# Four exact blocks of a Q piece instead of two, with the order of a slot rewritten on three engines

## The chip, the core and the metric

The kernel runs on one core of one Trainium2 chip. The metric is the device time of one launch in microseconds. A core has a tensor engine (TensorE, PE; its weight loads are PEld), a vector engine (VectorE, DVE), a scalar engine (ScalarE, ACT), GpSimd (POOL), and a sync engine (SyncE, SP) whose only work here is to issue DMAs. Each works through its own list of instructions in order and waits on semaphores.

## What is computed

One decoder layer with quantised weights on x of 2 x 512 x 1024:

```
x = x + attn(layernorm(x))      # 32 heads of 128, 8 KV heads, rope, causal softmax
                                # q, k, v, o weights: (codes - 8) * scales, one scale per 128 rows and column
x = x + fake_quant(layernorm(x)) @ fake_quant(ctx)    # ctx 2 x 1024 x 1024, 8 bit codes
x = x + layernorm(x) @ binarised(weight)              # sign(w) * mean|w| - clip(w) + clip(w)
```

A fp32 product is made of fp16 halves: each operand is split into an upper and a lower half, and three products (upper x upper, upper x lower, lower x upper) are summed. The codes minus 8 are small whole numbers and exact in one fp16. A product with unscaled codes therefore takes two matmuls instead of three, but its scale has to be applied to the result.

## The kernel before

Attention runs in 64 slots. A slot is one head and one batch row: p = 0 to 63, with i = p mod 8 inside the group g of one KV head, h = i // 2 the head and b = i % 2 the batch. The slots overlap as a pipeline written out by hand: in slot p the engines make the scores and the softmax of slot p, Q for slot p + 2, the weighted values of slot p - 1, and the output projection (O) of earlier heads. Every engine's list of a slot is one function called slot (POOL's is body), and the order of calls in it is the schedule. No scheduler stands between.

TensorE in a slot, in 128 x 512 matmuls: scores in three units u = 0, 1, 2 (3 + 3 + 1.5 columns' worth), Q for p + 2 from eight 128-row blocks, three units of O and one of the slot before (16 matmuls), and weigh, the product with V (7.5). For Q, q_exact multiplies with bare codes (2 matmuls), q_base lets ScalarE multiply the partial sum in PSUM by the ratio of this block's scale to the next one's, and so on; q_part adds the rest, each block with three matmuls of scaled halves. Two blocks are exact. The ratios stand in o_now, which o_scales copies from o_table; ratio_step computes the table once, in the K phase before the slots.

A piece of Q's weights is 128 x 512, half a head. It is loaded to stage_c (codes) and stage_s (scales broadcast). VectorE's piece_scale multiplies them, ScalarE's piece writes the upper half to w_a, VectorE's piece_lo the lower half. The exact columns of the first piece of a head need only (code - 8).

Q's result goes this way: ScalarE q_copy to SBUF, POOL q_turn (times cosine), ScalarE q_swap (two copies that exchange the partition halves), POOL sine, VectorE q_sum, ScalarE q_hi, POOL q_lo; then the scores can start.

The softmax of a slot: VectorE maxima after each score unit, ScalarE exps, VectorE two reciprocals (row_inv: three columns, then the fourth), POOL norm on four parts, ScalarE prob_split in two parts, POOL prob_rest, four transposing DMAs, TensorE weigh a slot later, ScalarE ao_part and VectorE ao_rest. O's results are added to x_acc by VectorE (o_add), four a slot; two PSUM tiles take turns, so a unit waits for the add two before it.

Beside that, slots 8 to 39 turn ctx into codes: ScalarE scales to uint8 and subtracts 128 in a second instruction. Slots 40 to 62 prepare the ffn weights (wf_upper and wf_sign on ScalarE, wf_lower and wf_difference on VectorE, wf_clip and wf_add on POOL). After slot 63 come the rest of O, the cross product and the ffn.

The groups 1 to 4 are a hardware loop on TensorE, VectorE, POOL and SP (each_group); on ScalarE they are written out.

## Time and profile before

| what | value |
|---|---|
| median of 3 runs | 1050.04 us (1050.01 to 1050.68) |
| profiled execution | 1050.22 us |
| its span | 1048.4 us |
| PE busy | 1015.7 us, 97%, 5296 matmuls |
| DVE busy | 902.7 us, 86% |
| POOL busy | 788.9 us, 75% |
| ACT busy | 774.4 us, 74% |
| granted TensorE clock | 1.000 |

The span is from the first to the last instruction of the profiled execution. A busy share says how much of the span an engine executed; it doesn't say where it is waited for. In the forty slices of the page TensorE has nine tenths or more in all but the first. Its slots lie between 168 us (first score product) and 895 us (last).

### The profile page before, as it was taken

The page shows a single profiled execution, that of the slowest core. Times are in us where ns is not written, and L with a number is a line of the kernel's source. Part 1 is how long each engine was busy: PE and PEld are TensorE (multiplying, and loading weights), DVE is VectorE, ACT ScalarE, POOL GpSimd, SP SyncE. Part 2 cuts the span into 40 slices and gives each one's busy share as a digit, 9 for nine tenths or more (in the row PEclk, how much of TensorE's full clock was granted, in tenths as well). Part 3 has the DMA queues.
Part 4 walks back from the last instruction along what each step waited for, and adds up shares of the span by engine and source line. Part 5 has one row for each costly group of instructions (what it writes and reads, how often), then busy time and mean ns, then how long its engine had stood idle before and what let it go on. Part 6 is the DMA issues. An engine that isn't in the chain of part 4 may idle for free.

```text
span 1048.4 us, 18487 instructions
## 1 busy us (share of the span) xinstructions
PE 1015.7 (97%) x5296; PEld 500.5 (48%) x5296; DVE 902.7 (86%) x1651; ACT 774.4 (74%) x1712; POOL 788.9 (75%) x833
## 2 busy tenths in 40 slices
PE   5999998999999999999999999999999999989998
PEld 3444343445555555555555455545555554454443
DVE  7989997699888888888888889999999998887773
ACT  5547766888898888888888888888888887473210
POOL 3678787899878887887888789999999999332200
PEclk9999999999999999999999999999999999999999
DMA  9783301676887676667667766777787765534442
GB/s 337 258 199 121 116 26 34 145 152 157 161 162 166 138 165 158 147 152 159 165 138 165 157 147 140 153 165 150 156 150 156 160 138 113 118 122 96 88 96 74
DMA packets 309804, 152.01 MB, mean 145 GB/s; under 512 B 257728, under 2 KB 274240, under 8 KB 309728
## 3 DMA queue, kind: packets, MB, share of 16 engines
q1 hardware_dynamic: 301952, 137.76, 58.0%
q10 hardware_dynamic: 7776, 13.37, 4.5%
q8 instruction: 31, 0.51, 0.2%
q14 instruction: 45, 0.37, 0.1%
HBM read 85.26 MB, written 4.19 MB: 85 GB/s over the span
## 4 chain that ended last, share of the span: by engine, by line
PE 82%; DVE 6%; POOL 5%; ACT 3%; issue 2%; DMA 1%; ACTq 0%; SPq 0%; DVEq 0%; POOLq 0%
PE out_ps L969 10%; PE proj_ps L969 9%; PE side_ps L949 9%; PE side_ps L757 8%; PE side_ps L759 8%; PE side_ps L758 8%; PE side_ps L845 5%; PE proj_ps L1130 5%; PE score_ps L932 3%; PE score_ps L933 3%; PE score_ps L934 3%; PE proj_ps L1135 2%; PE score_ps L1100 2%; PE out_ps L780 1%; PE proj_ps L757 1%
## 5 line engine op out<-in xcount | busy, mean ns | idle before, releaser
L1687 POOL TENSOR_SCALAR prob<-prob,row_inv 128x512 f32<-128x512 f32 (+3 forms) x256 | 196.7, 779 | 81.9 <-DVE row_inv L2224 80.3
L1694 POOL TENSOR_TENSOR w_b<-prob,w_b 128x896 f16<-128x896 f32 (+2 forms) x192 | 186.0, 995 | 6.5 <-ACT w_b L1373 6.4
L1346 ACT ACTIVATE prob<-score_ps,neg_max 128x512 f32<-128x512 f32 (+3 forms) x256 | 132.9, 526 | 30.7 <-DVE neg_max L2141 29.1
L2154 DVE SCALAR_TENSOR_TENSOR x_acc<-out_ps,o_now,x_acc 128x1024 f32<-128x1024 f32 x120 | 153.1, 1276 | 1.3 <-PE out_ps L969 1.3
L2154 DVE SCALAR_TENSOR_TENSOR x_acc<-proj_ps,o_now,x_acc 128x1024 f32<-128x1024 f32 x120 | 153.0, 1275 | 0.0
L757 PE MATMUL side_ps<-hT,w_a 128*128 128x512 f16 x384 | 145.5, 379 | 0.5 <-ACT side_ps L1313 0.2
L759 PE MATMUL side_ps<-hT,w_a 128*128 128x512 f16 x384 | 145.5, 379 | 0.0
L758 PE MATMUL side_ps<-hT,w_a 128*128 128x512 f16 x384 | 145.5, 379 | 0.0
L2141 DVE CUSTOM_DVE_ANT_0 score_ps<-score_ps,mask_b 128x512 f32<-128x512 f32 (+3 forms) x256 | 122.7, 501 | 16.9 <-PE score_ps L934 16.6
L969 PE MATMUL proj_ps<-work,w_b 128*128 128x512 f16 x496 | 127.3, 379 | 1.9 <-DVE x_acc L2154 1.5
L969 PE MATMUL out_ps<-work,w_b 128*128 128x512 f16 x496 | 127.3, 379 | 0.8 <-DVE x_acc L2154 0.7
L949 PE MATMUL side_ps<-work,v_sb 128*128 128x512 f16 (+3 forms) x768 | 114.8, 299 | 0.2 <-DMA work<-w_b 0.2
L1900 DVE SCALAR_TENSOR_TENSOR w_a<-stage_s,w_a 128x256 f16<-128x256 f32 (+1 forms) x64 | 64.7, 1010 | 43.4 <-ACT w_a L1216 43.1
L1373 ACT ACTIVATE w_b<-prob 128x896 f16<-128x896 f32 (+2 forms) x192 | 99.3, 550 | 3.6 <-POOL prob L1687 1.6
L1313 ACT ACTIVATE side_ps<-side_ps,o_now 128x512 f32<-128x512 f32 x120 | 79.3, 661 | 27.8 <-PE side_ps L845 24.3
L1682 POOL TENSOR_TENSOR swapped<-swapped,sin_t 128x512 f32<-128x512 f32 x77 | 99.7, 1295 | 0.0
L949 PEld LDWEIGHTS side_ps<-work,v_sb 128*128 128x128 f16 (+1 forms) x768 | 69.6, 98 | 45.3 <-DMA work<-w_b 1.2
L932 PE MATMUL score_ps<-k_sb,q_sb 128*128 (+4 forms) x256 | 76.7, 299 | 3.6 <-ACT prob L1346 2.0
L1707 POOL TENSOR_TENSOR q_sb<-rot,q_sb 128x512 f16<-128x512 f32 x62 | 78.9, 1273 | 0.0
L969 PEld LDWEIGHTS proj_ps<-work,w_b 128*128 128x128 f16 x496 | 48.2, 98 | 60.2 <-DVE x_acc L2154 2.5
L969 PEld LDWEIGHTS out_ps<-work,w_b 128*128 128x128 f16 x496 | 48.3, 98 | 59.7 <-DVE x_acc L2154 2.0
L933 PE MATMUL score_ps<-k_sb,q_sb 128*128 (+4 forms) x256 | 76.6, 299 | 0.0
(276 smaller groups left out, 2230.1 us busy)
## 6 DMA issues: line engine op xcount, KB each, us to landing
stage_c<-in_codes_dram SPq DMA_DIRECT2D x72, 256.0 KB, 2.9
stage_o<-in_codes_dram SPq DMA_DIRECT2D x64, 256.0 KB, 3.3
stage_s<-in_scales_dram SPq DMA_DIRECT2D x34, 256.0 KB, 3.7
ctx_raw<-in_ctx_dram ACTq DMA_DIRECT2D x32, 256.0 KB, 3.2
work<-w_b SPq DMA_TRANSPOSE x261, 3.1
x_acc<-in_x_dram SPq DMA_DIRECT2D x8, 512.0 KB, 8.9
k_sb<-in_codes_dram SPq DMA_DIRECT2D x16, 256.0 KB, 7.0
v_sb<-in_scales_dram SPq DMA_DIRECT2D x16, 256.0 KB, 7.4
```

The costliest lines, as they stand in the source:

```text
L757: pe.matmul(o, stat(0), mov(0), start=first, stop=False, skip_group_check=onto)
L758: pe.matmul(o, stat(0), mov(1), start=False, stop=False, skip_group_check=onto)
L759: return pe.matmul(o, stat(1), mov(0), start=False, stop=last, skip_group_check=onto)
L932: pe.matmul(o, q[0], k[0], start=True, stop=False)
L933: pe.matmul(o, q[0], k[1], start=False, stop=False)
L949: mm = pe.matmul(pv_ps[:, kb * P:S], v_sb[:, bass.ds(g, 1), l, b * TB + kb, :].rearrange("p a d -> p (a d)"), probT[:, m, at:kb + (TB - 1) ...
L969: mm = pe.matmul(o[:, b, :], o_codes[:, h % RING, cb * P:(cb + 1) * P], ao[:, h % 2, l, b * S:(b + 1) * S], start=l == 0, stop=l == 1)
L1346: ins = act.activation(prob[:, SCORE_AT[qb]:SCORE_AT[qb] + w], score_ps[:, score_bank(i, u), off:off + w], ACT.Exp, bias=neg_max[:, c:c + ...
L1687: return pool.tensor_scalar(prob[:, at:at + w], prob[:, at:at + w], row_inv[:, col:col + 1], P_UP, ALU.mult, ALU.mult)
L1694: ins = pool.tensor_tensor(prob16[:, 1, to:to + w], prob[:, at:at + w], prob16[:, 0, to:to + w], ALU.subtract)
L2141: ins = dve.tensor_tensor_reduce(s, s, mask_b[:, S - w:S], -1.0, MAX_FROM, ALU.add, ALU.min, neg_max[:, c:c + 1])
L2154: ins = dve.scalar_tensor_tensor(y, u, s, y, ALU.mult, ALU.add)
```

## The change

It raises the exact blocks of a Q piece from two to four in the slots whose Q is that of slots 10 to 63; TensorE makes it in slots 8 to 61 (the function many). An even piece is then whole: all of its 512 columns are exact, so it needs no scales, no piece_scale and no piece_lo. In these slots:

- TensorE: four q_exact of two matmuls, and q_part over four blocks instead of six. The first score unit is parted after its second product, the O units are parted at two, three or one of their four matmuls.
- ScalarE: four q_base instead of two; the second context instruction has gone to VectorE; the exchange of Q's halves is parted: one half at the end of a slot behind both prob_splits, the other after the next slot's first q_base. The last exponential comes behind the fourth q_base, q_hi and o_cut.
- VectorE: the first O add and q_sum stand ahead of the third maxima and of the first reciprocal; in the context slots a tensor_scalar from uint8 to bf16 behind the second reciprocal.
- SP: for a whole piece one load instead of two, and a wait on piece_hi instead of piece_done.
- Ratios: three columns of ratios instead of one, in six steps (14 instructions instead of 11), held in ctx_raw.
- The groups 1 to 4 are written out on every engine.

TensorE at the start of a context slot, from the first score product, before (side_ps<-hT,w_a is Q, score_ps the scores, out_ps and proj_ps the O units):

```order
L932 MATMUL score_ps<-k_sb,q_sb 128x512
L933 MATMUL score_ps<-k_sb,q_sb 128x512
L934 MATMUL score_ps<-k_sb,q_sb 128x512
L845 MATMUL side_ps<-hT,w_a 128x512 x2
L969 MATMUL out_ps<-work,w_b 128x512 x4
L932 MATMUL score_ps<-k_sb,q_sb 128x384
L933 MATMUL score_ps<-k_sb,q_sb 128x384
L934 MATMUL score_ps<-k_sb,q_sb 128x384
L932 MATMUL score_ps<-k_sb,q_sb 128x128
L933 MATMUL score_ps<-k_sb,q_sb 128x128
L934 MATMUL score_ps<-k_sb,q_sb 128x128
L845 MATMUL side_ps<-hT,w_a 128x512 x2
```

and now:

```order
L972 MATMUL score_ps<-k_sb,q_sb 128x512 x2
L884 MATMUL side_ps<-hT,w_a 128x512 x2
L972 MATMUL score_ps<-k_sb,q_sb 128x512
L1008 MATMUL out_ps<-work,w_b 128x512 x4
L884 MATMUL side_ps<-hT,w_a 128x512 x2
L972 MATMUL score_ps<-k_sb,q_sb 128x384 x3
L972 MATMUL score_ps<-k_sb,q_sb 128x128 x3
L1008 MATMUL proj_ps<-work,w_b 128x512 x2
L884 MATMUL side_ps<-hT,w_a 128x512 x2
L1008 MATMUL proj_ps<-work,w_b 128x512 x2
L1008 MATMUL out_ps<-work,w_b 128x512 x3
L884 MATMUL side_ps<-hT,w_a 128x512 x2
```

The exact pairs (two matmuls to side_ps) went from two to four; between each pair and the next stand five 512-wide matmuls or as much.

VectorE from the first score unit's O add to the first reciprocal, in the weight stage before, an odd slot (ISA is the maxima instruction and its accumulator read, rot<-rot,swapped is q_sum, x_acc an O add):

```order
L2154 SCALAR_TENSOR_TENSOR x_acc<-out_ps,o_now,x_acc 128x1024
L2141 ISA score_ps,neg_max<-score_ps,mask_b 128x384
L2141 ISA neg_max 128x1
L2141 ISA score_ps,neg_max<-score_ps,mask_b 128x128
L2141 ISA neg_max 128x1
L2141 ISA score_ps,neg_max<-score_ps,mask_b 128x256
L2141 ISA neg_max 128x1
L2154 SCALAR_TENSOR_TENSOR x_acc<-proj_ps,o_now,x_acc 128x1024
L2224 RECIPROCAL row_inv<-row_sum 128x3
L2054 TENSOR_TENSOR rot<-rot,swapped 128x512
```

and in a context slot now; in the weight stage these rows are the same:

```order
L2250 SCALAR_TENSOR_TENSOR x_acc<-out_ps,o_now,x_acc 128x1024
L2237 ISA score_ps,neg_max<-score_ps,mask_b 128x384
L2237 ISA neg_max 128x1
L2237 ISA score_ps,neg_max<-score_ps,mask_b 128x128
L2237 ISA neg_max 128x1
L2250 SCALAR_TENSOR_TENSOR x_acc<-proj_ps,o_now,x_acc 128x1024
L2145 TENSOR_TENSOR rot<-rot,swapped 128x512
L2237 ISA score_ps,neg_max<-score_ps,mask_b 128x256
L2237 ISA neg_max 128x1
L2324 RECIPROCAL row_inv<-row_sum 128x3
```

The second O add and q_sum moved ahead of the third maxima (128x256) and the reciprocal.

ScalarE from the second probability split to the first scaling of the next slot's Q, before (an odd slot follows; swapped<-stage_o is half of the exchange, w_b<-prob the split, work<-side_ps the ao copy, side_ps<-side_ps q_base):

```order
L1221 ACTIVATE swapped<-stage_o 64x512
L1222 ACTIVATE swapped<-stage_o 64x512
L1373 ACTIVATE w_b<-prob 128x128
L1373 ACTIVATE w_b<-prob 128x256
L1382 ACTIVATE work<-side_ps 128x512
L1329 ACTIVATE o_now<-work 128x10
L1432 DMA ctx_raw<-in_ctx_dram 128x512
L1313 ACTIVATE side_ps<-side_ps,o_now 128x512
```

and now:

```order
L1447 ACTIVATE w_b<-prob 128x128
L1447 ACTIVATE w_b<-prob 128x256
L1370 ACTIVATE swapped<-stage_o 64x512
L1456 ACTIVATE work<-side_ps 128x512
L1506 DMA ctx_raw<-in_ctx_dram 128x512
L1387 ACTIVATE side_ps<-side_ps,o_now 128x512
L1370 ACTIVATE swapped<-stage_o 64x512
L1387 ACTIVATE side_ps<-side_ps,o_now 128x512
```

One half of the exchange stands between the second split and the ao copy, the other between the first and the second q_base; before, both stood ahead of the second split.

The diff, cut to its core:

```diff
-N_EXACT = 2
-EXACT = N_EXACT * P
+N_EXACT = 4
+FEW_EXACT = 2
+MANY = range(SLOTS + Q_AHEAD, N_SLOTS)
+def exact_of(p):
+    return N_EXACT if p in MANY else FEW_EXACT
+def whole(n):
+    return exact_columns(n) == PIECE
+        def many(p):
+            return p + Q_AHEAD in MANY
...
         def each_group(eng, body):
             body(0)
-            with eng.Fori(1, CTX_GROUPS + 1) as g:
+            for g in range(1, CTX_GROUPS + 1):
                 body(g, True)
...
+                if exact == PIECE:
+                    return
                 sp.dma_start(stage_s[:, r, exact:PIECE],
...
-                    sp.wait_ge(piece_done, p + FIRST_PIECES)
+                    of = p + FIRST_PIECES - 1
+                    sp.wait_ge(*((piece_hi, of + 1) if whole(of) else (piece_done, halved(of + 1))))
...
+                if many(p):
+                    scores(p, i, g, 0, range(2))
+                    q_exact(*ahead, 0)
+                    scores(p, i, g, 0, range(2, 3))
+                    o_unit(p - 1, prev[1], 3)
+                    q_exact(*ahead, 1)
+                    scores(p, i, g, 1)
+                    o_unit(p, i, 0, range(0, 2))
+                    q_exact(*ahead, 2)
+                    o_unit(p, i, 0, range(2, 4))
+                    o_unit(p, i, 1, range(0, 3))
+                    q_exact(*ahead, 3)
+                    o_unit(p, i, 1, range(3, 4))
+                    scores(p, i, g, 2)
+                    o_unit(p, i, 2, range(0, 2))
+                    q_part(*ahead, range(N_EXACT, KB))
+                    o_unit(p, i, 2, range(2, 4))
+                    weigh(p - 1, prev[1], prev[0])
+                    return
...
+                if whole(n):
+                    act.activation(w[:, 0, col:col + PIECE], stage_c[:, r, :], ACT.Copy, bias=-CODE_ZERO)\
+                        .then_inc(piece_hi, 1)
+                    return
...
+            def q_swap_half(p, half):
+                if half == 0:
+                    act.wait_ge(q_summed, p)
+                    act.wait_ge(q_copied, p - FIRST_PIECES + 1)
+                a, z = half * 64, half * 64 + 64
+                ins = act.activation(swapped[a:z, :], q_sum_in[64 - a:128 - a, :], ACT.Copy)
+                if half:
+                    ins.then_inc(q_swapped, 1)
...
+                if many(p):
+                    if many(p - 1):
+                        q_swap_half(p - 1 + Q_AHEAD, 1)
                     q_base(*next_q, 1)
+                    exps(p, i, 0)
+                    if i % B:
+                        o_scales(g, i)
+                    q_base(*next_q, 2)
+                    exps(p, i, 1)
+                    q_base(*next_q, 3)
                     q_hi(p + 1)
+                    o_cut(p, i)
+                    if wf_late(p) is not None:
+                        wf_upper(wf_late(p))
+                    exps(p, i, 2)
+                    if with_ctx:
+                        act.wait_ge(ctx_landed, q * 16 + 16)
+                        act.activation(ctx_codes, ctx_raw[:, :], ACT.Identity, scale=scal[:, 5:6],
+                                       bias=scal[:, 3:4]).then_inc(ctx_scaled, 1)
...
                 prob_split(p, 1)
+                if many(p):
+                    q_swap_half(p + Q_AHEAD, 0)
+                    if not many(p + 1):
+                        q_swap_half(p + Q_AHEAD, 1)
...
+                    dve.tensor_tensor(per[:, :, 0], rows[:, :, 0], per[:, :, 0], ALU.mult)
+                    ins = dve.tensor_tensor(per[:, :, 1:], by[:, :, 0:N_EXACT - 2], per[:, :, 1:], ALU.mult)
...
                 maxima(p, i, 1)
-                maxima(p, i, 2)
-                if has_o:
+                if many(p):
                     if i % B:
                         dve.wait_ge(o_now_ready, g * RF + i // B)
                     o_add(p, i, 0)
-                dve.wait_ge(exp_done, p * 3 + 2)
-                dve.reciprocal(row_inv[:, 0:3], row_sum[:, 0:3]).then_inc(inv_ready[0], 1)
-                if has_next and by_parts(p + 1):
                     q_sum(p + 1)
+                maxima(p, i, 2)
+                if many(p):
+                    dve.wait_ge(exp_done, p * 3 + 2)
+                    dve.reciprocal(row_inv[:, 0:3], row_sum[:, 0:3]).then_inc(inv_ready[0], 1)
...
-                if has_piece:
-                    piece_scale(n, i % 2, (EXACT, 0)[i % B])
+                if has_piece and not whole(n):
+                    piece_scale(n, i % 2, exact)
                 dve.wait_ge(exp_done, p * 3 + 3)
                 dve.reciprocal(row_inv[:, 3:4], row_sum[:, 3:4]).then_inc(inv_ready[1], 1)
+                if with_ctx:
+                    q, dst = ctx_half(g, i)
+                    dve.wait_ge(ctx_scaled, q + 1)
+                    dve.tensor_scalar(dst, ctx_codes, Q_MID, None, ALU.subtract).then_inc(ctx_free, 1)
```

## Rows read from the trace of the kernel before

**Rows 1.** Windows view, the context stage; busy us of each engine, clock, DMA.
```profile
466.00:558.00 92.00, 92.00 (x499) 46.71 (x498) 78.01 (x145) 81.62 (x186) 76.18 (x81) 1.00 0.68 155
```

**Rows 2.** Timeline of TensorE: start us, us, engine, line, operation, tiles.
```profile
697.72 0.38 PE L932 MATMUL score_ps<-k_sb,q_sb 128*128 128x512 f16 x1
709.18 0.38 PE L932 MATMUL score_ps<-k_sb,q_sb 128*128 128x512 f16 x1
510.97 1.03 PE L969 MATMUL out_ps<-work,w_b 128*128 128x512 f16 x4
```

**Rows 3.** Timeline of ScalarE, context stage; last row a group, mean ns.
```profile
508.11 0.48 ACT L1346 ACTIVATE prob<-score_ps,neg_max 128x256 f32<-128x256 f32 x1
508.56 0.82 ACT L1453 ACTIVATE ctx_raw<-ctx_raw,scal 128x512 uint8<-128x512 f32 x1
509.73 0.63 ACT L1321 ACTIVATE q_sb<-rot 128x512 f16<-128x512 f32 x1 [0.35 <-DVE rot L2054]
511.78 0.93 ACT L1373 ACTIVATE w_b<-prob 128x896 f16<-128x896 f32 x1
512.74 0.63 ACT L1221 ACTIVATE swapped<-stage_o 64x512 f32<-64x512 f32 x1
514.03 0.62 ACT L1373 ACTIVATE w_b<-prob 128x128 f16<-128x128 f32 x2
514.56 0.58 ACT L1382 ACTIVATE work<-side_ps 128x512 f16<-128x512 f32 x1
L1313 ACT ACTIVATE side_ps<-side_ps,o_now 128x512 f32<-128x512 f32 x64 | 42.4, 662 | 16.0 <-PE side_ps L845 12.5
```

**Rows 4.** Timeline of VectorE, context stage.
```profile
503.79 0.69 DVE L2170 SCALAR_TENSOR_TENSOR work<-side_ps,work 128x512 f16<-128x512 f32 x1 [0.40 <-ACT work L1382]
506.94 0.14 DVE L2141 DVE_READ_ACCUMULATOR2_ANT neg_max<- 128x1 f32 x1
507.40 0.43 DVE L2141 CUSTOM_DVE_ANT_0 score_ps<-score_ps,mask_b 128x256 f32<-128x256 f32 x1 [0.32 <-PE score_ps L934]
507.75 0.14 DVE L2141 DVE_READ_ACCUMULATOR2_ANT neg_max<- 128x1 f32 x1
509.03 0.66 DVE L2054 TENSOR_TENSOR rot<-rot,swapped 128x512 f32<-128x512 f32 x1
509.61 0.68 DVE L1894 SCALAR_TENSOR_TENSOR stage_s<-stage_c,stage_s 128x512 f32<-128x512 int32 x1
521.07 0.42 DVE L1894 SCALAR_TENSOR_TENSOR stage_s<-stage_c,stage_s 128x256 f32<-128x256 int32 x1
```

**Rows 5.** Timeline of POOL, an odd slot and the even one after it.
```profile
509.28 2.05 POOL L1687 TENSOR_SCALAR prob<-prob,row_inv 128x512 f32<-128x512 f32 x2 [2.24 <-DVE row_inv L2224]
511.30 1.15 POOL L1707 TENSOR_TENSOR q_sb<-rot,q_sb 128x512 f16<-128x512 f32 x1
513.67 2.90 POOL L1694 TENSOR_TENSOR w_b<-prob,w_b 128x896 f16<-128x896 f32 x3
520.75 1.78 POOL L1687 TENSOR_SCALAR prob<-prob,row_inv 128x512 f32<-128x512 f32 x2 [1.71 <-DVE row_inv L2224]
524.60 1.89 POOL L1694 TENSOR_TENSOR w_b<-prob,w_b 128x896 f16<-128x896 f32 x1
```

**Rows 6.** Groups of POOL, the two slots' first norm.
```profile
L1687 POOL TENSOR_SCALAR prob<-prob,row_inv 128x512 f32<-128x512 f32 x1 | 1.5, 1487 | 2.2 <-DVE row_inv L2224 2.2
L1687 POOL TENSOR_SCALAR prob<-prob,row_inv 128x512 f32<-128x512 f32 x1 | 1.2, 1220 | 1.7 <-DVE row_inv L2224 1.7
```

**Rows 7.** Groups of VectorE over the span.
```profile
L2080 DVE TENSOR_SCALAR q_ratio<-q_ratio 128x32 f32<-128x32 f32 x1 | 1.2, 1245 | 0.0
```

**Rows 8.** Groups of VectorE in the weight stage.
```profile
L2101 DVE SCALAR_TENSOR_TENSOR w_b<-w_b,wf_mean 128x256 f32<-128x256 f32 x15 | 19.3, 1289 | 0.0
L2107 DVE SCALAR_TENSOR_TENSOR w_b<-w_b 128x256 f16<-128x256 f32 x14 | 10.6, 758 | 0.0
L1900 DVE SCALAR_TENSOR_TENSOR w_a<-stage_s,w_a 128x512 f16<-128x512 f32 x7 | 6.6, 944 | 0.0
```

More of the change, by code:

```diff
@@ L59 @@
 Q_AHEAD = 2
-N_EXACT = 2
-EXACT = N_EXACT * P
+N_EXACT = 4
+FEW_EXACT = 2
+RATIO_STEPS = 6
 Q_LEAD = 3
@@ L852, in q_part @@
                 p = g * SLOTS + i
-                first = N_EXACT if by_parts(p) else 0
+                first = exact_of(p) if by_parts(p) else 0
                 if known(p) and p < Q_AHEAD and kbs[0] % 4 == 0:
@@ L1025, in slot @@
                 if has_ahead:
-                    q_part(*ahead, range(N_EXACT if parts else 3, KB))
+                    q_part(*ahead, range(exact_of(p + Q_AHEAD) if parts else 3, KB))
                 if has_o:
@@ L2081, in ratio_step @@
                 elif k == 2:
-                    ins = dve.tensor_tensor(by, by, rows[:, :, 1], ALU.add)
+                    ins = dve.tensor_tensor(by, by, of, ALU.add)
                 elif k == 3:
@@ L2181, in slot @@
                 n = p + FIRST_PIECES
+                exact = 0 if i % B else exact_columns(n)
                 p_ge2 = not (known(p) and p < 2)
```

172 lines of the change are left out of this document (95 added, 77 removed).

## The prediction, made before the result was known

> **What bounds the kernel now.** I read the table of windows first, because busy shares over the whole span mix stages. From 466 to 558 us, inside the context stage, TensorE is busy for 92.00 of 92.00 us and the granted clock is 1.00, which is the 2.4 GHz level; ScalarE stands at 81.62 and POOL at 76.18 [rows 1]. Then I read TensorE's timeline for the step of a slot: the first score product of one slot starts at 697.72, the next at 709.18, so a slot is 11.46 us [rows 2]. That is in the weight stage; in the context stage POOL's first norms stand as far apart (509.28 and 520.75) [rows 5]. Four matmuls issued in a row show as 1.03 us, of which the last one's own 0.38 is a modelled end, so a 512-wide matmul costs a step of (1.03 - 0.38) / 3 = 0.215 us [rows 2]. The slots are bound by TensorE's issue, and whatever goes from it comes back in full only if nobody else needs more than the shorter slot.
>
> **TensorE's part.** A block from exact codes takes two matmuls, any other three. Four instead of two exact blocks in 54 slots removes 54 x 2 matmuls: 108 x 0.215 = 23.2 us, 0.43 a slot, so a slot of pure issue would be 11.03 us. Each further exact block adds a scaling in place by ScalarE between two pairs of matmuls: 0.66 us [rows 3]. The new TensorE order puts five matmuls' worth (1.07 us) between the pairs, enough for the drain of the pair before (about 0.2 more than its issue) and 0.66, with about 0.1 to 0.2 us over. So the ladder costs nothing if ScalarE comes to each scaling on time. That is the condition to examine.
>
> **ScalarE's part.** In the window ScalarE is busy 81.62 / 92 x 11.46 = 10.17 us a slot [rows 1]. It gains 2 x 0.66, loses the second context copy (a step of 0.51, below) and, in half the slots, about 0.1 for a piece that is now one instruction instead of two: 10.9 of 11.03. It hardly has room to wait, and now it must wait for TensorE four times a slot. Beside that its half swap stands behind the second splitting of the probabilities: 0.63 [rows 3].
>
> **The loop that closes through VectorE, POOL and ScalarE.** I follow one round of an odd context slot, from ao_rest on VectorE to the ao_rest a slot later.
> Before: ao_rest, first maxima, O add, second maxima take 503.79 to 506.94 = 3.15, third maxima 0.35 (507.40 to 507.75), the next O add 1.20 (507.75 to 509.03, less the 0.08 of the reciprocal between): 4.70 [rows 4]. From there the reciprocal and its semaphore take 0.33 until POOL's first norm at 509.28 (0.08 to q_sum at 509.03, 0.25 more). POOL goes from that norm at 509.28 to the first subtraction at 513.67: 4.39 [rows 5]. ScalarE's second split takes 0.53 (514.03 to 514.56), the ao copy 0.58, semaphores 0.07 [rows 3]. Sum 10.60, which is 0.86 under the slot: nobody sees it.
> After: q_sum stands ahead of the third maxima and the reciprocal, +0.60 (0.66 less the usual overlap of 0.06) [rows 4]. The half swap stands between the split and the ao copy, +0.63, and +0.10 because a row before a swap keeps its full step (split at 511.78, 0.93 long, swap only at 512.74) [rows 3]. On the other side POOL's first norm no longer meets q_sum: q_sum ran until 509.69, so 0.41 of it lay on the norm, -0.41. Sum 11.52 for an odd slot. In an even slot, whose piece is whole, piece_scale and piece_lo are gone: POOL's stretch was already 0.54 shorter there (520.75 to 524.60 = 3.85) [rows 5] and loses 0.33 more of the scaling (from 521.16, where q_sum must end if it repeats the slot before, to 521.49) and, an estimate, 0.17 of piece_lo: 10.48, to which the new VectorE copy adds up to 0.5. The two kinds alternate. An even slot is then set by TensorE (11.03) or ScalarE's own round: q_sum's end at 3.15 + 1.20 + 0.66 = 5.01, four short copies (q_hi, o_cut, q_cut, q_copy) at the step of 0.51 that the four instructions from 509.73 to 511.78 show (2.05), exponential 0.45 (508.11 to 508.56), context scaling 0.73 (0.82 less an overlap of 0.1), splits 0.85 and 0.62, swap 0.63, ao 0.58: 10.92 [rows 3, 4]. Mean (11.52 + 11.03) / 2 = 11.28, and rounds that cross from one chain into the other can only lengthen it. I take 11.35 for the 32 slots with context, with 11.03 and 11.75 as ends.
>
> **Why I subtract port time.** The same norm of 128x512 took 1487 ns in one slot and 1220 in the next [rows 6]. The slots differ by VectorE's scaling of 512 or 256 columns (0.68 and 0.42 us, at 509.61 and 521.07 [rows 4]), and the difference of the norms, 267 ns, is that of the scalings. So POOL stands still while such a VectorE instruction runs. The Trainium skill ("GPSIMD Engine Reference", Key points) says that the two share SBUF interfaces and collide where VectorE has two SBUF inputs or a two-port mode; by that rule, the trace agrees: q_sum and the scalings have two SBUF inputs, and the O adds, one from PSUM, do no harm. The moved context copy has one SBUF source, so the rule catches it only in a two-port mode.
> The trace speaks for catching it: a tensor_scalar on 32 columns in SBUF took 1245 ns [rows 7], where 256 columns elsewhere take 0.42: it stood behind something as long as a two-input instruction of POOL (q_lo: 1.15 [rows 5]). The copy itself isn't in the trace of before. Its bounds: 0.42, the 256-wide row, and 1.8 us, 0.66 (q_sum, as wide) behind a q_lo of 1.15; I take 0.5. It hides behind the wait for the third exponential unless caught.
>
> **The 22 slots with ffn weights (40 to 61).** Here VectorE's in-order round counts. Front to q_sum's end 5.01 [rows 4]. Then the fourth part of the exponentials, which now stands behind q_hi: two short copies 1.02, wf_upper 0.35 (an estimate, from copies twice as wide at 0.51), exponential 0.48 with about 0.08 for its accumulator, semaphores 0.1: 7.04. VectorE waits for it at the second reciprocal (0.08), and only then does wf_lower 0.76, piece_lo 0.94 in half the slots (0.47), wf_diff 1.29 [rows 8], two O adds 2.40: 12.04. These durations contain waits for POOL; with 0.42 for each 256-wide one (the scaling of that width) and 0.66 for the lo they would give 10.69, below TensorE's 11.03. POOL is as loaded as before and its q_lo still falls on wf_lower, but wf_diff now meets short norms. I take 11.70, with ends 11.03 and 12.04.
>
> **The rest.** SP loads no scale rows for whole pieces: fewer transfers, and its transposes issue as before. The table of ratios makes 14 small VectorE instructions where there were 11, in a phase where VectorE is nearly full; the one of 1245 ns waited some 1.1 us for POOL [rows 7], and the steps go from seven to six: between -1 and +2, I take +0.5. Filling and leaving the stage: +0.5. That four engines' loops are written out costs nothing: the slots at 697 us are already straight code and have the same 11.46 step [rows 2].
>
> **Sum.** 32 x (11.35 - 11.46) = -3.5; 22 x (11.70 - 11.46) = +5.3; +1.0: +2.8 us. The profiled execution took 1050.2 (span 1048.4 and 1.8 around it), the median of the runs is 1050.04, so the two can be set equal: 1053 us. With 11.35 +- 0.12 and 11.70 +- 0.2 this case reaches from 1046 to 1061.
>
> **Rivals.**
> 1. TensorE stays the bound. For it: all loops have slack of 0.9 us or more before, and the even slots lose 0.9 us of VectorE work. Against it: the additions to the loop alone are 1.33. If every slot is 11.03, 1050.2 - 23.2 = 1027; if only the odd ones stay at 11.2 to 11.5, 1033 to 1045.
> 2. Slower outright, by one mechanism: VectorE, which comes late from the exponential, meets POOL's q_lo (1.15 us) with a port-holding instruction in each slot, the moved copy in the context slots, wf_lower in the others, and hands the lateness to the O adds and to ao_rest. Then context slots are 11.75 and weight slots 12.04: 32 x 0.29 + 22 x 0.58 = +22, 1072 us. It decides from the point where the second reciprocal starts after POOL has begun q_lo. By the Trainium skill's page named above this is what a two-port copy must do; by the rows it is open.
> 3. The gains meet the losses exactly: context slots at 11.2 and weight slots at 11.8 give -8.3 + 7.5 + 1 = 0, 1050. It lies inside the first case's range.
>
> **Chances.** The forecast with the third rival, 1046 to 1061: 0.50. Rival 1, 1027 to 1046: 0.31. Rival 2, above 1061: 0.19. Less than 0.2% (2.1 us) can't be told from no change. Of the forecast's 0.50, 0.06 is faster than 1048, 0.17 lies within 1047.9 to 1052.1, 0.27 above. So faster 0.37, same 0.17, slower 0.46. The range leaves out about one in ten on each side: 1037 to 1065.
>
> **What would show it.** In the profile after, TensorE should have holes of 0.1 to 0.7 us in the slots, most before the second exact pair (waiting for ScalarE's scaling of side_ps) or before an O unit (waiting for an O add of VectorE), and few in slots 0 to 7. The slot steps should alternate, or average 11.35 in the context stage and 11.7 in the weight stage. POOL's first norm should be nearer 0.7 than 1.22 us in even slots. VectorE should wait 1 us or more for the third exponential. I am wrong if TensorE is whole between 283 and 830 us (rival 1), or if the weight slots are no longer than the context slots. If the copy of the context codes on VectorE lasts over 1 us, rival 2's mechanism is there.

## The result, and the profile after

The changed kernel takes 1064.01 us (median of 4 runs, 1063.71 to 1064.15) beside 1050.24 for the kernel before on the same chip: a ratio of 1.013 with a 95% interval of 1.012 to 1.014. It is 1.3% slower. The prediction said 1053, with 1037 to 1065. The profiled execution has a span of 1062.4.

First the windows. The columns are window, length, then busy time and instructions of PE, PEld, DVE, ACT and POOL, granted clock, DMA share, GB/s. The first is the stretch of [rows 1], the second lies in the stage with ffn weights.

```profile
466.00:558.00 92.00, 89.68 (x484) 43.49 (x482) 78.27 (x145) 86.56 (x190) 73.07 (x81) 1.00 0.65 149
650.00:742.00 92.00, 86.53 (x462) 41.18 (x460) 79.46 (x143) 82.46 (x188) 78.85 (x94) 1.00 0.66 146
```

Where before TensorE was busy for all 92 us, it now lacks 2.3 in the context stage and 5.5 in the weight stage, at an unchanged clock of 1.00. (Over the whole page before, three slices besides the first stand at eight tenths, not nine; none of them lies inside these windows.) It no longer sets the slots. Its timeline says where the holes are: ahead of the second pair of exact matmuls, waiting for ScalarE's scaling in place.

```profile
518.32 0.61 PE L884 MATMUL side_ps<-hT,w_a 128*128 128x512 f16 x2 [0.58 <-ACT side_ps L1387]
...
715.88 0.60 PE L884 MATMUL side_ps<-hT,w_a 128*128 128x512 f16 x2 [0.71 <-ACT side_ps L1387]
```

The step of a slot can be read on ScalarE's ao copy, which comes once a slot. Five starts in the changed kernel, three of them in the context stage:

```profile
505.19 0.57 ACT L1456 ACTIVATE work<-side_ps 128x512 f16<-128x512 f32 x1
...
517.00 0.57 ACT L1456 ACTIVATE work<-side_ps 128x512 f16<-128x512 f32 x1
...
528.09 0.57 ACT L1456 ACTIVATE work<-side_ps 128x512 f16<-128x512 f32 x1
...
702.62 0.57 ACT L1456 ACTIVATE work<-side_ps 128x512 f16<-128x512 f32 x1
...
714.56 0.57 ACT L1456 ACTIVATE work<-side_ps 128x512 f16<-128x512 f32 x1
```

Context slots are 11.81 (odd) and 11.09 (even) in turn, 11.45 on average, where [rows 2, 5] had 11.46. Weight slots are 11.94 here and 12.07 for the next, 12.00 on average, against 11.46. Before slot 2 the ao copy already starts 1.9 us later (194.16 for 192.24). Followed through all ao copies, the lag behind the kernel before is 2.4 us at the end of slot 7, 2.3 at the end of slot 39, 13.6 at the end of slot 61 and 13.9 at the last one. So of the 14 us 11.3 come from the 22 weight slots, 1.9 from the phase that computes K with 0.4 in the slots just behind it, 0.3 from the end, and nothing from the 32 context slots. 22 x 0.54 would be 11.9; slot 40 is still 11.08, slot 60 is 11.45, and slot 61, the last of them, is 12.76 against 11.46.

What delays the scaling in an even weight slot is seen when the three other engines are laid side by side. VectorE, POOL and ScalarE from 708 us:

```profile
708.67 0.17 DVE L2324 RECIPROCAL row_inv<-row_sum 128x3 f32<-128x3 f32 x1
710.39 0.16 DVE L2339 RECIPROCAL row_inv<-row_sum 128x1 f32<-128x1 f32 x1 [1.54 <-ACT prob L1420]
710.47 1.20 DVE L2203 SCALAR_TENSOR_TENSOR w_b<-w_b 128x256 f16<-128x256 f32 x1
712.21 0.48 DVE L2197 SCALAR_TENSOR_TENSOR w_b<-w_b,wf_mean 128x256 f32<-128x256 f32 x1 [0.54 <-ACT w_b L1482]
```

```profile
709.01 1.25 POOL L1778 TENSOR_SCALAR prob<-prob,row_inv 128x512 f32<-128x512 f32 x2 [1.22 <-DVE row_inv L2324]
710.23 1.16 POOL L1798 TENSOR_TENSOR q_sb<-rot,q_sb 128x512 f16<-128x512 f32 x1
711.36 0.99 POOL L1778 TENSOR_SCALAR prob<-prob,row_inv 128x128 f32<-128x128 f32 x2
```

```profile
711.76 0.42 ACT L1482 ACTIVATE w_b<-w_b 128x256 f32<-128x256 f32 x1 [0.89 <-DVE w_b L2203]
712.08 0.58 ACT L1377 ACTIVATE stage_o<-side_ps 128x512 f32<-128x512 f32 x1
712.56 1.44 ACT L1447 ACTIVATE w_b<-prob 128x896 f16<-128x896 f32 x3
714.03 0.63 ACT L1370 ACTIVATE swapped<-stage_o 64x512 f32<-64x512 f32 x1
714.56 0.57 ACT L1456 ACTIVATE work<-side_ps 128x512 f16<-128x512 f32 x1
715.16 0.66 ACT L1387 ACTIVATE side_ps<-side_ps,o_now 128x512 f32<-128x512 f32 x1
```

wf_lower (L2203) starts 0.24 after POOL's q_lo (L1798) and ends only behind it: 1.20 us. ScalarE's next instruction, wf_sign (L1482), waits 0.89 for it, and behind wf_sign stand q_copy, the splits, the half swap, the ao copy and the scaling for which TensorE waits. The VectorE row at 712.21, wf_diff, was 1289 ns in [rows 8] and is 0.48 now: the contention has moved from it to wf_lower, where somebody waits.

In the context stage the odd and the even slot differ on POOL. The first and second batch of norms of an odd slot, then of an even one:

```profile
511.65 1.53 POOL L1778 TENSOR_SCALAR prob<-prob,row_inv 128x512 f32<-128x512 f32 x2 [2.09 <-DVE row_inv L2324]
...
514.28 1.51 POOL L1778 TENSOR_SCALAR prob<-prob,row_inv 128x128 f32<-128x128 f32 x2
...
523.40 1.25 POOL L1778 TENSOR_SCALAR prob<-prob,row_inv 128x512 f32<-128x512 f32 x2 [2.29 <-DVE row_inv L2324]
...
525.75 1.00 POOL L1778 TENSOR_SCALAR prob<-prob,row_inv 128x128 f32<-128x128 f32 x2
```

The second batch takes 0.5 longer in the odd slot. VectorE's new context copy reaches 0.3 us into it in both slots; what only the odd slot has is piece_lo, which lies wholly inside it:

```profile
513.42 1.16 DVE L2343 TENSOR_SCALAR v_sb<-ctx_raw 128x512 bf16<-128x512 uint8 x1 [0.54 <-ACT ctx_raw L1526]
514.50 0.68 DVE L1991 SCALAR_TENSOR_TENSOR w_a<-stage_s,w_a 128x512 f16<-128x512 f32 x1
...
525.17 0.88 DVE L2343 TENSOR_SCALAR v_sb<-ctx_raw 128x512 bf16<-128x512 uint8 x1 [0.54 <-ACT ctx_raw L1526]
```

Between 283 and 550 us the 24 copies lasted 1023 ns on average. Before 128 us, VectorE's third scaling of a piece and the wide reciprocal of the ratio table:

```profile
115.86 0.74 DVE L2174 RECIPROCAL ctx_raw<-ctx_raw 128x96 f32<-128x96 f32 x1
...
125.26 1.64 DVE L1985 SCALAR_TENSOR_TENSOR stage_s<-stage_c,stage_s 128x512 f32<-128x512 int32 x1
```

In the trace of before, that reciprocal on 32 columns took 0.34 and that scaling 0.67. Not all of the lag comes from there. VectorE's first rot<-rot,swapped, at 74.00 us before, stands at 74.45 now, ahead of the first step of the table, and between 73.96 and 74.66 in the traces of e1, e2, e8, e9 and e11. So 0.45 of the 1.9 is an earlier difference, not the table's.

### The profile page after: what moved, and what is told of

It is laid out like the page before. It is cut to its first block, busy times and chain, and to the rows that moved or that the text cites. A ratio compares the mean times of both kernels' runs of the same rounds, so it can differ in the third digit from the quotient of the medians.

```text
span 1062.4 us, 17456 instructions
## 1 busy us (share of the span) xinstructions
PE 1004.0 (95%) x5188; PEld 478.0 (45%) x5188; DVE 891.1 (84%) x1632; ACT 816.8 (77%) x1761; POOL 760.2 (72%) x833
## 4 chain that ended last, share of the span: by engine, by line
PE 48%; DVE 17%; ACT 12%; issue 11%; POOL 9%; ACTq 1%; DMA 1%; DVEq 0%; SPq 0%; POOLq 0%
PE proj_ps L1008 6%; PE side_ps L884 6%; PE score_ps L972 5%; PE proj_ps L1190 5%; POOL prob L1778 4%; PE side_ps L988 4%; PE out_ps L1008 4%; DVE x_acc L2250 3%; PE side_ps L796 2%; PE side_ps L798 2%; PE side_ps L797 2%; PE proj_ps L1195 2%; DVE score_ps L2237 2%; PE score_ps L1160 2%; DVE rot L2145 2%
## 5 line engine op out<-in xcount | busy, mean ns | idle before, releaser
L1778 POOL TENSOR_SCALAR prob<-prob,row_inv 128x512 f32<-128x512 f32 (+3 forms) x256 | 171.9, 682 | 103.2 <-DVE row_inv L2324 96.7
L1387 ACT ACTIVATE side_ps<-side_ps,o_now 128x512 f32<-128x512 f32 x228 | 150.9, 662 | 8.6 <-PE side_ps L884 3.5
L884 PE MATMUL side_ps<-hT,w_a 128*128 128x512 f16 x456 | 136.3, 381 | 22.4 <-ACT side_ps L1387 22.3
L972 PE MATMUL score_ps<-k_sb,q_sb 128*128 128x512 f16 (+3 forms) x768 | 144.6, 299 | 4.8 <-ACT prob L1420 3.8
L1008 PE MATMUL proj_ps<-work,w_b 128*128 128x512 f16 x496 | 145.9, 381 | 1.5 <-DVE x_acc L2250 1.5
L1008 PE MATMUL out_ps<-work,w_b 128*128 128x512 f16 x496 | 136.3, 380 | 2.0 <-DVE x_acc L2250 0.7
L796 PE MATMUL side_ps<-hT,w_a 128*128 128x512 f16 x276 | 104.5, 379 | 0.5 <-ACT side_ps L1387 0.2
L798 PE MATMUL side_ps<-hT,w_a 128*128 128x512 f16 x276 | 104.6, 379 | 0.0
L797 PE MATMUL side_ps<-hT,w_a 128*128 128x512 f16 x276 | 104.6, 379 | 0.0
L972 PEld LDWEIGHTS score_ps<-k_sb,q_sb 128*128 128x128 f16 x768 | 71.8, 98 | 65.4 <-ACT prob L1420 6.8
L988 PEld LDWEIGHTS side_ps<-work,v_sb 128*128 128x128 f16 x768 | 70.0, 98 | 46.1 <-issue 1.4
L884 PEld LDWEIGHTS side_ps<-hT,w_a 128*128 128x128 f16 x456 | 39.7, 97 | 86.6 <-ACT side_ps L1387 64.3
L1793 POOL TENSOR_TENSOR rot<-stage_o,cos_t 128x512 f32<-128x512 f32 x60 | 76.2, 1271 | 0.0
```

The costliest lines, as they stand in the source:

```text
L797: pe.matmul(o, stat(0), mov(1), start=False, stop=False, skip_group_check=onto)
L798: return pe.matmul(o, stat(1), mov(0), start=False, stop=last, skip_group_check=onto)
L884: mm = pe.matmul(q_ps, w_a[:, 0, w:w + P], hT[:, l, e, i % B * S:(i % B + 1) * S], start=l + e == 0, stop=l == 1, skip_group_check=e > 0)
L972: mm = pe.matmul(o, q[n // 2], k[n % 2], start=n == 0, stop=n == 2)
L988: mm = pe.matmul(pv_ps[:, kb * P:S], v_sb[:, bass.ds(g, 1), l, b * TB + kb, :].rearrange("p a d -> p (a d)"), probT[:, m, at:kb + (TB - 1) ...
L1008: mm = pe.matmul(o[:, b, :], o_codes[:, h % RING, cb * P:(cb + 1) * P], ao[:, h % 2, l, b * S:(b + 1) * S], start=l == 0, stop=l == 1)
```

## Experiments

Three theories stood against each other. P: the weight slots are long because wf_lower meets q_lo and ScalarE waits for it. R: all slots hang on the release of POOL's first norm, which now stands behind q_sum and the third maxima. T: the late third part of the exponentials, on which the prediction's round for the weight slots turned, is the cause. The expectations have letters of their own: theory A is T in e3 and R in e4; in e1 it says only that the loss is in the weight slots, and theory P in e6 is about the context copy. Every ratio is to the kernel before as it ran beside the experiment. Those medians lie between 1050.24 and 1050.82, so a difference of two experiments is good to about 1 us.

**e1_context_slots_only.** The range of blocks with four exact parts is cut at 42.

```diff
-MANY = range(SLOTS + Q_AHEAD, N_SLOTS)
+MANY = range(SLOTS + Q_AHEAD, 42)
```

> Four exact blocks and the new orders only in the 32 context slots (8 to 39); the weight slots 40 to 61 keep the orders of before. Theory A (the loss is in the weight slots: 22 x about 0.54 us, plus about 2 us from the phase that computes K): 1064 - 12 = 1052 us. Theory B (the loss arises where TensorE's new order waits for ScalarE's scaling, whatever the slot, so context slots lose their share too): about 0.26 us a slot, 1058 us. Theory C (with every slot of the context stage bound as before, only the way out of it matters): 1050 or less.

Measured: 1053.12 us, ratio 1.002 (1.001 to 1.003). Its context slots are 11.82 and 11.08, its weight slots 11.65 and 11.28 as before. So 10.9 us of the 13.8 are in the weight slots (11.4 by the two ratios), and the stages add up. Where the loss lies is shown by this, not why.

**e2_no_slot.** MANY is empty, the context copy ScalarE's.

```diff
-MANY = range(SLOTS + Q_AHEAD, N_SLOTS)
+MANY = range(0)
```

> No slot has four exact blocks or the new orders; the context copy is ScalarE's again. What is left of the change is the table of ratios with 96 columns instead of 32 and loops written out. Theory A (the shift of some 2 us that the trace shows before slot 8 comes from the table's steps, which push VectorE's two-input scalings onto POOL's instructions): 1052. Rival (the shift comes from the slots' own entry): 1050.0 to 1050.5.

Measured: 1052.65 us, ratio 1.0015 (1.0005 to 1.0024); the first ao copy starts at 194.11. What lies ahead of the slots costs 1.9 us, of which the difference at 74 us is a part. All later slots have the steps of before, so loops written out cost nothing.

**e3_third_exp_early.** ScalarE's order in slots 8 to 61:

```diff
-                    q_hi(p + 1)
                     o_cut(p, i)
+                    exps(p, i, 2)
+                    q_hi(p + 1)
                     if wf_late(p) is not None:
                         wf_upper(wf_late(p))
-                    exps(p, i, 2)
```

> As the changed kernel, but ScalarE does the third part of the exponentials right behind o_cut, ahead of q_hi and wf_upper, so VectorE's second reciprocal comes about 1 us earlier. Theory A (VectorE's in-order round, waiting 1.0 to 1.5 us for that exponential, sets the weight slots at 12.0): they fall to 11.2 to 11.5, which is 22 x 0.5 to 0.8 = 11 to 18 us, and the context slots fall little: 1046 to 1053. Rival (the round through POOL's norms and ScalarE's second split sets them; the exponential's lateness is idle time that another wait takes over): 1062 to 1065.

Measured: 1064.17 us, ratio 1.012 (1.011 to 1.014): no gain. Theory T fell. The reciprocal did come earlier, but wf_lower then waited for wf_upper, which stood behind, and still fell on q_lo (VectorE, POOL, ScalarE of an even weight slot):

```profile
709.03 0.16 DVE L2339 RECIPROCAL row_inv<-row_sum 128x1 f32<-128x1 f32 x1 [0.60 <-ACT prob L1420]
709.85 1.39 DVE L2203 SCALAR_TENSOR_TENSOR w_b<-w_b 128x256 f16<-128x256 f32 x1 [0.66 <-ACT w_b L1489]
```

```profile
709.81 1.16 POOL L1798 TENSOR_TENSOR q_sb<-rot,q_sb 128x512 f16<-128x512 f32 x1
```

```profile
711.34 0.42 ACT L1482 ACTIVATE w_b<-w_b 128x256 f32<-128x256 f32 x1 [1.00 <-DVE w_b L2203]
```

My edit had moved the wait, not removed it, so it says against T only that an earlier exponential alone is worth nothing; it does not clear it as one of two conditions.

**e4_recip_early.** VectorE's order:

```diff
                     o_add(p, i, 0)
+                    dve.wait_ge(exp_done, p * 3 + 2)
+                    dve.reciprocal(row_inv[:, 0:3], row_sum[:, 0:3]).then_inc(inv_ready[0], 1)
                     q_sum(p + 1)
                 maxima(p, i, 2)
-                if many(p):
-                    dve.wait_ge(exp_done, p * 3 + 2)
-                    dve.reciprocal(row_inv[:, 0:3], row_sum[:, 0:3]).then_inc(inv_ready[0], 1)
```

> As the changed kernel, but VectorE's first reciprocal stands ahead of q_sum and of the third maxima, so POOL's first norm is released about 0.9 us earlier (and meets q_sum for 0.4 again). Theory A for the odd context slots (11.81, the loop of ao_rest, norms, second split, half swap): they lose about 0.5 to 0.7, the even ones nothing, 16 x 0.6 = 10 us; the weight slots, set by the third exponential, lose under 0.2: 1051 to 1055. Rival (context slots are set by ScalarE's own queue, not by POOL): 1062 to 1065.

Measured: 1050.33 us, ratio 0.9996 (0.9986 to 1.0005). This one reorder gives back the whole loss. The odd context slots fell from 11.81 to 11.33 and the even ones rose to 11.16; the weight slots, of which I had expected less than 0.2, went from 12.07 and 11.94 to 11.83 and 11.40. R holds in both stages, because POOL's earlier norms also take q_lo out of wf_lower's way in the even slots (VectorE, ScalarE):

```profile
702.50 0.16 DVE L2338 RECIPROCAL row_inv<-row_sum 128x1 f32<-128x1 f32 x1 [1.57 <-ACT prob L1420]
702.58 0.47 DVE L2203 SCALAR_TENSOR_TENSOR w_b<-w_b 128x256 f16<-128x256 f32 x1
```

```profile
703.14 0.42 ACT L1482 ACTIVATE w_b<-w_b 128x256 f32<-128x256 f32 x1 [0.15 <-DVE w_b L2203]
```

VectorE waits as long for the third exponential as it did (1.57), and the slot is 0.54 shorter. The edit moves the reciprocal ahead of q_sum and of the third maxima at once; no run separates the two.

**e5_lower_first.** VectorE does wf_lower ahead of its second reciprocal:

```diff
+                if many(p) and wf_late(p) is not None:
+                    wf_lower(wf_late(p))
                 dve.wait_ge(exp_done, p * 3 + 3)
                 dve.reciprocal(row_inv[:, 3:4], row_sum[:, 3:4]).then_inc(inv_ready[1], 1)
...
-                if known(p) and wf_late(p) is not None:
+                if not many(p) and wf_late(p) is not None:
                     wf_lower(wf_late(p))
```

> As the changed kernel, but in slots 8 to 61 VectorE does wf_lower ahead of its second reciprocal instead of behind it, so that it need not wait for the third part of the exponentials. Theory P (the weight slots stand at 12.0 because wf_lower falls on POOL's q_lo, 1.2 us instead of 0.4, and ScalarE's wf_sign, with q_copy, the splits, the half swap and the first scaling behind it, waits 0.9 for it in the even slots): the weight slots fall to 11.5 to 11.7, 1053 to 1057 us. Theory R (they are set by the release of POOL's first norm alone, which this leaves as it is): 1063 to 1065. The context slots have no wf_lower and stay at 11.45 on average.

Measured: 1055.86 us, ratio 1.005 (1.003 to 1.007). Even weight slots fell from 11.94 to 11.12, odd ones stayed (12.09), and context slots did not move. This is P by itself: POOL's first norm starts 5.63 us behind ao_rest as it did, and wf_lower no longer ends behind q_lo. Nine even slots and slot 61, at 0.82 each, are the 8.2 us that are back. The row shows 0.60 for 1.20, ScalarE no longer waits at wf_sign, and it is q_lo that is longer (1.32 for 1.16):

```profile
708.25 0.60 DVE L2203 SCALAR_TENSOR_TENSOR w_b<-w_b 128x256 f16<-128x256 f32 x1 [1.09 <-ACT w_b L1489]
```

**e6_context_copy_scalare.** The context copy back on ScalarE, and out of VectorE's list:

```diff
+                        act.wait_ge(ctx_scaled, q + 1)
+                        act.activation(dst, ctx_codes, ACT.Copy, bias=-Q_MID).then_inc(ctx_free, 1)
...
-                if with_ctx:
-                    q, dst = ctx_half(g, i)
-                    dve.wait_ge(ctx_scaled, q + 1)
-                    dve.tensor_scalar(dst, ctx_codes, Q_MID, None, ALU.subtract).then_inc(ctx_free, 1)
```

> As the changed kernel, but the second instruction of a context tile (codes to bf16) is ScalarE's again in every context slot. VectorE loses 1.02 us a slot, ScalarE gains 0.5 to 0.6. Theory P (the copy on VectorE holds the port: POOL's second batch of norms takes 1.51 us in odd slots, 1.00 in even ones): odd slots lose 0.3 to 0.5, even slots, where ScalarE is nearly full, gain 0.3 to 0.5: 1061 to 1066 us. If the copy is what costs, odd slots 11.3 and even 11.1: 1056. If ScalarE's load is what costs, every slot 11.6: 1069.

Measured: 1073.33 us, ratio 1.022 (1.020 to 1.024). Every context slot is 11.70 to 11.77, and ScalarE's busy time from 283 to 550 us is 257.70 of 267. All three lines of my expectation were off, the last one least: ScalarE's load is what costs. VectorE is the better place for the copy. This run also says what the copy did to POOL: without it the second batch of norms takes 1.36 in an odd slot and 0.84 in an even one, for 1.51 and 1.00, so the copy holds POOL up by 0.15 in both, and the 0.5 between the two kinds stays. It is piece_lo's.

**e7_half_swap_behind_base.** The half swap that stood before the ao copy stands behind the first scaling of the next slot, the other behind the second:

```diff
                     if many(p - 1):
-                        q_swap_half(p - 1 + Q_AHEAD, 1)
+                        q_swap_half(p - 1 + Q_AHEAD, 0)
                     q_base(*next_q, 1)
+                    if many(p - 1):
+                        q_swap_half(p - 1 + Q_AHEAD, 1)
...
                 if many(p):
-                    q_swap_half(p + Q_AHEAD, 0)
                     if not many(p + 1):
+                        q_swap_half(p + Q_AHEAD, 0)
                         q_swap_half(p + Q_AHEAD, 1)
```

> As the changed kernel, but the first half of Q's swap stands behind the first scaling of the next slot, the second half behind the second scaling, so the split, the ao copy and the first scaling follow one another. ScalarE's work is the same, the loop through VectorE and POOL loses 0.63. Theory R (that loop sets the odd context slots and the weight slots): odd context slots 11.81 to about 11.2, weight slots 12.0 to 11.4 to 11.6: 1064 - 16 x 0.6 - 22 x 0.5 = 1043 to 1048. Rival (ScalarE's own in-order round sets them): 1061 to 1065.

Measured: 1068.92 us, ratio 1.017 (1.015 to 1.018), slower. Context slots 11.27 and 11.89. ScalarE came to the scalings too early and to the exponentials too late: it now waited for TensorE's pairs, and o_scales (o_now<-work, the table row for the O units), which stands behind the first exponentials, was late for VectorE's O add.

```profile
507.86 0.66 ACT L1387 ACTIVATE side_ps<-side_ps,o_now 128x512 f32<-128x512 f32 x1 [0.27 <-PE side_ps L884]
...
509.37 0.66 ACT L1387 ACTIVATE side_ps<-side_ps,o_now 128x512 f32<-128x512 f32 x1 [0.20 <-PE side_ps L884]
```

```profile
511.62 1.28 DVE L2252 SCALAR_TENSOR_TENSOR x_acc<-proj_ps,o_now,x_acc 128x1024 f32<-128x1024 f32 x1 [0.61 <-ACT o_now L1403]
```

A loop shortened on paper by 0.63 became longer: what left ScalarE's queue ahead of the ao copy came back into it ahead of the exponentials.

**e8_recip_and_exp_early.** e4, and on ScalarE o_cut, wf_upper, the third exponential, q_hi, in this order:

```diff
-                    q_hi(p + 1)
                     o_cut(p, i)
                     if wf_late(p) is not None:
                         wf_upper(wf_late(p))
                     exps(p, i, 2)
+                    q_hi(p + 1)
```

> Both: VectorE's first reciprocal ahead of q_sum and the third maxima, as in e4, and on ScalarE o_cut, wf_upper, the third exponential, then q_hi. With e4 alone ScalarE still waited 0.37 for q_sum at q_hi and 0.15 to 0.58 for wf_lower at wf_sign in weight slots of 11.40 and 11.83. Theory A (these waits are ScalarE's only holes there and its round sets the slot): weight slots 11.0 to 11.3, context slots 11.1 to 11.2: 1050.3 - 22 x 0.4 - 32 x 0.1 = 1037 to 1042. Rival (as with the early exponential alone, another wait takes the place): 1049 to 1051.

Measured: 1042.59 us, ratio 0.992 (0.990 to 0.994). Slots of 11.08 and 11.39 in the context stage, 11.08 and 11.44 in the weight stage. So the exponential's place is worth 7.7 us once the first norm is released early, and nothing before that (e3, whose order differs by wf_upper).

**e9_q_lo_last** and **e10_one_norm_ahead.** Both are built on e8. POOL's order, and the start of the table of ratios (RATIO_FROM 8 instead of 4). In e10 only norm(0) is moved ahead of q_lo.

```diff
                     norm(2).then_inc(norm_done, 1)
-                    q_lo(p + 1)
                     norm(0)
                     pool.wait_ge(inv_ready[1], p + 1)
                     norm(1).then_inc(norm_done, 1)
+                    q_lo(p + 1)
```

> As e8 with two more edits: POOL does q_lo behind all four norms instead of behind the second (slots 8 to 61), and the six steps of the table of ratios start four steps later in the phase that computes K, where VectorE waits 0.3 to 0.9 us for POOL in each step. In e8 the odd slots stood at 11.39 to 11.44 with POOL waiting 0.2 to 0.5 for ScalarE's q_hi and ScalarE waiting 0.20 to 0.25 for POOL's last norm. Theory A (the last norm, and with it the second split, is what makes the odd slots longer than 11.08): odd slots 11.08 to 11.2, 27 x 0.25 = 7 us less. The table's move: the first ao copy, at 193.9 to 194.2 in the runs with the table's steps in their place and 192.2 in the kernel before, at 192.7 to 193.3, 1 us less. Together 1042.6 - 8 = 1034 to 1037. Rival (q_lo, now later, makes the next first score wait, or falls on piece_lo and wf_lower): 1042 to 1048.

> As e9, but only the short norm of 128 columns goes ahead of q_lo, into the hole in which POOL waits for q_hi; the last norm stays behind q_lo. Theory A: the norms end 0.2 to 0.3 earlier than in e8, odd slots 11.15 to 11.25: 1036 to 1039. Rival (the holes at q_hi are not on the path): as e8 with the table moved, 1041 to 1042.

Measured: 1046.83 and 1046.94 us, ratio 0.9965 (0.9951 to 0.9979) for both. The table's move was a miss: the first ao copy at 195.37 and 195.39, 1.5 later instead of 1 earlier; the reason is not known. In e9 the weight slots came to 11.08 and 11.19 to 11.27, as theory A said, but every second context step to 11.68 (by the ao copies it is the one from an odd slot to the next even one). There piece_lo, in the odd slot, fell on q_lo and pushed both O adds:

```profile
514.11 1.47 DVE L1994 SCALAR_TENSOR_TENSOR w_a<-stage_s,w_a 128x512 f16<-128x512 f32 x1
```

e10 has 11.30 and 11.13 in the context stage, and 11.26 and 11.66 in the weight stage.

**e11_q_lo_last_piece_lo_late.** e9 with the table in its place, and in odd context slots:

```diff
-                if has_piece and not whole(n):
+                lo_late = with_ctx and many(p)
+                if has_piece and not whole(n) and not lo_late:
                     piece_lo(n, i % 2, q_region(i), Q_UP, exact)
...
                     o_add(p, i, 1)
+                    if has_piece and not whole(n) and lo_late:
+                        piece_lo(n, i % 2, q_region(i), Q_UP, exact)
                     o_add(p, i, 2)
```

> As e9, with the table's steps back where they were (their move cost 1.5 us at the first ao copy, where 1 us less was expected), and in odd context slots VectorE's piece_lo behind the first of its two O adds instead of ahead of both. In e9 the weight slots came to 11.08 and 11.21, but the odd context slots to 11.68, where piece_lo fell on the later q_lo: 1.47 us, with both O adds and ao_rest behind it. Theory A (only that meeting costs): odd context slots 11.08 to 11.25; 1042.6 - 32 x 0.12 - 22 x 0.12 = 1035 to 1038. Rival (VectorE's own queue is full in odd slots and the place of piece_lo does not matter): 1044 to 1046.

Measured: 1037.41 us, ratio 0.9875 (0.9859 to 0.9892): 1.25% faster than the kernel before, 26.6 us faster than the changed kernel. Context slots are 11.08 odd and even, weight slots 11.08 and 11.19 to 11.28. piece_lo is 0.68 again, and TensorE is full in the weight stage:

```profile
507.93 0.68 DVE L1994 SCALAR_TENSOR_TENSOR w_a<-stage_s,w_a 128x512 f16<-128x512 f32 x1
```

```profile
283.00:550.00 267.00, 264.75 (x1435) 129.25 (x1433) 230.31 (x429) 256.62 (x561) 220.54 (x240) 1.00 0.68 154
650.00:842.00 192.00, 192.00 (x1032) 93.28 (x1031) 175.57 (x329) 184.40 (x424) 184.38 (x208) 1.00 0.68 154
```

The 2.25 us that TensorE lacks in the first window are 0.58 in one slot at 344 and 1.67 in one at 533. What follows in each can be read, what starts it can't. In the slot at 344 of e4, e8, e9, e10 and e11 VectorE stands still for 0.28 ahead of q_sum, with nothing in the profile that it waits for; q_sum then falls on POOL's first norm (1.11 for 0.66), and the slot is 0.7 to 0.8 longer than its kind. (e2 has a slot there that is 0.6 longer by another way, a wait of ScalarE for a transpose, and gets most of it back in the next.) At 533 VectorE is 0.15 later than two slots before, and the context copy begins 0.09 behind q_lo instead of 0.06 ahead of it. It takes 1.35 instead of 0.43, piece_lo then falls on POOL's prob_rest, and TensorE waits for it:

```profile
528.71 1.35 DVE L2345 TENSOR_SCALAR v_sb<-ctx_raw 128x512 bf16<-128x512 uint8 x1 [1.06 <-ACT ctx_raw L1526]
531.18 1.85 DVE L1994 SCALAR_TENSOR_TENSOR w_a<-stage_s,w_a 128x512 f16<-128x512 f32 x1
```

```profile
533.08 0.61 PE L884 MATMUL side_ps<-hT,w_a 128*128 128x512 f16 x2 [1.67 <-DVE w_a L1994]
```

So the order of e11 rests on a lead of 0.06 us.

## Why the prediction was right and where it was not

**Slower: right, but the size was five times what I gave** (+2.8 predicted, +13.8 measured). 1064 lies above the forecast's own case (1046 to 1061), in the share of 0.19 that I had given to rival 2, and 1 us inside the range. That it is still inside is luck. The term that was mis-sized most is the weight slots; the context slots were 3.5 us too low.

- **Weight slots.** The round came to 12.04 with the durations of before and 10.69 without contention; I took 11.70 because wf_diff "now meets short norms". It does: counted to the next start, that row took 0.46 on average where 1.29 stood. But the round of two slots from 703.38 to 727.39 is 12.00 a slot, because as much came in elsewhere: 0.27 a slot in which VectorE waits for wf_sign (0.54 in even slots; [rows 8] had none), 0.26 from piece_lo (1.53 for 0.94, in half the slots), 0.14 up to the second reciprocal, 0.07 with the O adds. wf_lower, 1.20 in even slots and 0.41 in odd ones, is 0.80 on average for 0.76, hardly more than before; what is new is which slot it is long in, and who waits. The term is 11.3 instead of 5.3. Rival 2's mechanism, VectorE meeting q_lo with wf_lower, is what e5 isolates in the even slots, and its 12.04 was nearer than my 11.70.
- **A link was missing.** I took the round to be VectorE's own. ScalarE's wf_sign waits for wf_lower, and q_copy to the scaling wait behind wf_sign; in the trace of before it waited for it only 1.6 us in all over 17 slots, and I left it out. I also put the cause on the late exponential. VectorE does wait for it as I said (1.54 and 0.97 us in weight slots, 1.24 in even context slots, 0.66 in odd ones), but e3 shows that its lateness alone is worth nothing, and e8 that it costs once the first norm comes early.
- **The loop through POOL.** Right in kind: q_sum ahead of the reciprocal was the +0.60 of the sum, and e4, which takes it back together with the 0.35 of the third maxima, is worth 13.7 us. Even context slots were predicted at 11.03 and are 11.08; odd ones at 11.52 and are 11.81. The round of the odd slot from ao_rest at 505.79 shows where the 0.3 is. 0.23 stands ahead of VectorE's O add, where I had no wait: its maxima are through by 508.93, but the second half of TensorE's O unit, which now stands behind the third exact pair, ends only at 509.06.

```profile
508.46 0.60 PE L1008 MATMUL proj_ps<-work,w_b 128*128 128x512 f16 x2
```

```profile
508.93 0.14 DVE L2237 DVE_READ_ACCUMULATOR2_ANT neg_max<- 128x1 f32 x1
509.17 1.28 DVE L2250 SCALAR_TENSOR_TENSOR x_acc<-proj_ps,o_now,x_acc 128x1024 f32<-128x1024 f32 x1
```

  Another 0.13 is POOL's stretch, 4.11 (511.65 to 515.76) where I had 3.98: the second batch of norms took 1.51 where 1.26 stood before, because the context copy pushes piece_lo wholly into it; I had added the copy to the round of the even slots only. Mean 11.45 for 11.35, a term of 0 instead of -3.5.
- **The context copy on VectorE.** Taken at 0.5, between 0.42 and 1.8; measured 1.02. The sign that I named for rival 2 in the context stage (over 1 us) came true, but its price did not: the slots are 11.45, not 11.75, since the even slots stay at 11.09. VectorE waits 1.24 us for the third exponential there and 0.54 for the scaled codes, and 0.25 for the ao copy behind it, so most of the copy lies in slack. That it waits for POOL at all is, by the Trainium skill ("GPSIMD Engine Reference", Key points), what a two-port mode of VectorE would do; the traces agree in that the copy took 0.43 us in e11 where it began ahead of POOL's q_lo and 1.35 where it began 0.09 behind the start of q_lo, and no run shows the mode itself.
- **The K phase.** Taken at +0.5 with -1 to +2, measured +1.9 (e2 and the first ao copy), of which 0.45 was there before the table began. About 1.0 is the third scaling, which starts 0.64 later and falls on a POOL instruction (1.64 for 0.67). The reciprocal is 0.4 longer, but VectorE's next wait for POOL, at 121 us, is shorter by as much (0.30 for 0.70).
- **TensorE, ladder and unrolled loops.** The pure slot of 11.03 is reached to within 0.05 in most slots of e11, with four scalings in each, so the ladder costs nothing when ScalarE is on time, and the loops written out cost nothing (e2). The holes before the second exact pair are where the prediction put them. POOL's first norm was to come near 0.7 us in even slots: it took 691 ns in the one at 523.40 and 966 in the odd one before it, where 1220 and 1487 stood in [rows 6].
- **Rival 1** (TensorE remains the bound) was false for this order, and is nearly true of e11.

## What to carry to other kernels

Price a reorder by who stands behind the moved instruction on the other engines, not by its length: one reciprocal of 0.08 us placed behind 1 us of work decided 13.7 us here. Where instructions of two engines lengthen each other, as VectorE's and POOL's do here, move an instruction that somebody waits for out of the other's long one; the total of contention may stay, as long as it falls on rows nobody waits for. Such an order can hang on little: in e11 a lead of 0.06 us decides whether the copy takes 0.43 or 1.35. And test an early release together with the one that hides it: the exponential's place was worth 0 alone and 7.7 us with the reciprocal's.
